# Layer 3 of a four-layer hybrid begins on image 0 before the layer ahead of it is done, without the dummy image

## What is computed

```python
x = x + _L0_conv_ref(_gn(x), ...)
x = x + _L1_conv_ref(_gn(x), ...)
t = _to_tokens(x)
t = t + _L2_attn_ref(_ln_t(t), L2_attn_w_attn, L2_attn_w_proj)
t = t + _L2_ffn_ref(_ln_t(t), L2_ffn_W1, L2_ffn_b1, L2_ffn_W2, L2_ffn_b2)
t = t + _L3_attn_ref(_ln_t(t), L3_attn_qkv_w, L3_attn_qkv_b, L3_attn_out_w, L3_attn_out_b)
t = t + _L3_ffn_ref(_ln_t(t), ...)
```

```python
for g in range(NUM_GROUPS):
    ag = x[g * gs:(g + 1) * gs]
    gamma = jnp.max(jnp.abs(ag))
    xq = xq.at[g * gs:(g + 1) * gs].set(jnp.clip(ag * QB / (gamma + EPS), -QB + EPS, QB - EPS))
```

## Time and profile before

| what | us |
|---|---|
| median of 3 runs | 804.9 |
| lowest and highest of them | 804.72 and 805.72 |
| the profiled execution | 806.04 |
| its span in the trace | 803.8 |
| PE busy | 743.9 (93%) |
| DVE busy | 578.1 |
| ACT busy | 571.6 |
| POOL busy | 253.1 |

### The profile page before, as it was taken

One profiled execution on the slowest core, in us unless ns is written; L12 is line 12 of the kernel. 1 busy time (PEld: TensorE's weight loads), 2 busy tenths in 40 slices (PEclk: granted clock), 3 DMA queues, 4 the chain that ended last, 5 costly groups with the idle time before them and its releaser, 6 DMA issues.

```text
span 803.8 us, 16948 instructions
## 1 busy us (share of the span) xinstructions
PE 743.9 (93%) x5265; PEld 583.6 (73%) x5265; DVE 578.1 (72%) x1415; ACT 571.6 (71%) x1425; POOL 253.1 (31%) x485
## 2 busy tenths in 40 slices
PE   1896999999999888999998986999999999999997
PEld 1874788788788776777776585677777786777775
DVE  6238677676777567788886798688888735877775
ACT  3323777977777557888886866688888748788785
POOL 1902155565554332121222000131212100544434
PEclk9999899999999999999999998899999959999999
DMA  6000000110110132333230002133333102223220
GB/s 218 1 1 0 1 7 17 20 16 18 20 17 16 26 90 74 90 90 104 80 103 17 0 1 80 51 99 88 102 94 89 29 1 82 50 59 76 63 50 20
DMA packets 60073, 41.36 MB, mean 51 GB/s; under 512 B 33904, under 2 KB 52464, under 8 KB 59888
## 3 DMA queue, kind: packets, MB, share of 16 engines
q1 hardware_dynamic: 60016, 40.63, 19.9%
HBM read 12.24 MB, written 3.21 MB: 19 GB/s over the span
## 4 chain that ended last, share of the span: by engine, by line
PE 77%; DVE 11%; ACT 4%; issue 3%; DMA 2%; SPq 2%; POOL 1%; POOLq 0%; DVEq 0%; ACTq 0%
PE ps L1236 11%; PE ps L990 10%; PE ps L1403 9%; PE ps L1418 8%; PE ps L1091 6%; PE ps L995 5%; PE ps L1075 3%; PE ps L1019 3%; PE ps L1033 3%; PE ps L998 2%; PE ps L1020 2%; SPq L309 2%; DMA qk<-hl 2%; PE ps L940 2%; DVE amax L1861 2%
## 5 line engine op out<-in xcount | busy, mean ns | idle before, releaser
L625 ACT ACTIVATE ee<-ps,nmax 128x128 f32<-128x128 f32 (+1 forms) x576 | 205.2, 445 | 11.5 <-DVE nmax L1592 6.4
L1236 PE MATMUL ps<-w,ee 128*128 128x128 f32 x960 | 134.8, 274 | 2.0 <-ACT big L612 1.9
L1236 PEld LDWEIGHTS ps<-w,ee 128*128 128x128 f32 x960 | 112.8, 143 | 13.6 <-ACT ee L625 2.8
L612 ACT ACTIVATE big<-ps 128x512 f32<-128x512 f32 (+1 forms) x192 | 96.6, 555 | 24.7 <-PE ps L1236 23.0
L1595 DVE TENSOR_REDUCE nmax<-ps 128x2 f32<-128x256 f32 x192 | 97.5, 550 | 13.5 <-PE ps L998 8.9
L1716 DVE TENSOR_TENSOR hhl<-ee,hhl 128x512 fp32r<-128x512 f32 x96 | 79.1, 829 | 33.1 <-ACT hhl L859 31.6
L990 PE MATMUL ps<-kh,big 128*128 128x256 f32 x384 | 94.7, 391 | 1.5 <-POOL big L385 1.2
L1592 DVE TENSOR_REDUCE nmax<-ps 128x4 f32<-128x1024 f32 x48 | 58.7, 1224 | 45.3 <-PE ps L990 45.1
L1403 PE MATMUL ps<-qk,w1hl 128*128 128x512 f32 x288 | 85.4, 405 | 0.0
L1418 PE MATMUL ps<-hhl,w2hl 128*96 128x512 f32 x288 | 82.4, 396 | 2.2 <-DVE big L1946 1.9
L529 POOL TENSOR_TENSOR xc<-big,xc 96x512 f32<-96x512 f32 x32 | 52.1, 1628 | 100.0 <-DVE big L1946 99.4
(11 more groups left out here) (260 smaller groups left out, 1333.2 us busy)
## 6 DMA issues: line engine op xcount, KB each, us to landing
qk<-hl SPq DMA_DIRECT2D x256, 96.0 KB, 3.1
big<-moe_gate SPq DMA_DIRECT2D x8, 768.0 KB, 6.9
w<-w_in SPq DMA_DIRECT2D x1, 1735.0 KB, 12.5
xc<-x_in SPq DMA_DIRECT2D x4, 384.0 KB, 5.6
l_mix<-on SPq DMA_DIRECT2D x32, 48.0 KB, 2.1
tok<-l_mix SPq DMA_DIRECT2D x16, 96.0 KB, 2.0
out<-xc SPq DMA_DIRECT2D x8, 192.0 KB, 2.1
w<-w_in SPq DMA_DIRECT2D x1, 998.0 KB, 8.8
```

The source lines that it names most:

```text
L612: nc.scalar.activation(et[:, h, 0:w], ps[:, 4 + hh, 0:w], ACT.Copy).then_inc(own(l, f"et{hh}"), 1)
L625: last = nc.scalar.activation(ee[:, ke, hh, qc, 0:w], src, ACT.Exp, bias=nmax[:, kp, hh, qc:qc + 1])
L1236: last = nc.tensor.transpose(ps[:, 4 + hh, b * P:(b + 1) * P], ee[:, u, hh, qc, tc * P:(tc + 1) * P], ident)
```

## The change

1. The five groups need not be through when layer 3 begins. Channels are now transposed and copied by 4 tiles (512 tokens, m = 0 to 7) rather than by half a group: m = 0 needs group 0 alone. m = 0 and 1 go through banks 0 and 1, the later ones all through bank 6. Steps of late groups are moved into layer 3's first units (`F2_LATE_PE`, `F2_LATE_ACT`, `F2_LATE_DVE`, by unit k): the quantise step of group 4 (f4) is in unit 0 on DVE, n4 in unit 2, the norms and roots of groups 3 and 4 on ACT in units 0 and 1, transposes m = 2 to 7 in units 0, 1, 2, 3 and 5.
2. The dummy image is gone in layers 2 and 3; its steps only count their semaphores up. So are the two matmuls that filled bank 6.
3. Image 0 of layer 3 is restacked by two queues: SP issues 4 of the 8 DMAs, ACT the other 4 (step D0, between the root and the norm of group 1).
4. The second matmul's results have banks of their own (`Y2_BANKS`), so that it waits for earlier ones only in group 4.
5. POOL begins `stage` in layer 3 once two pieces of `xn` are there, and does the cast and subtraction of `w2hl` after four images rather than two. Its all-reduces have a list of their own.

```diff
-F2_PE = ["h0", "h1", "h2", "h3", "h4", "y0", "y1", "y2", "y3", "T0", "Q0", "y4", "T1", "Q1", "S0", "T2", "S1", "T3", "V0", "T4"]
-F2_ACT = [..., "L0", "R0", "N0", "R1", "C0", "N1", "Q0", "R2", "N2", "C1", "Q1", "R3", "N3",
-          "C2", "R4", "X0", "C3", "C4"]
-F2_DVE = [..., "y0", "q4", "f0", "y1", "b0", "f1", "y2", "b1", "f2", "k0", "y3", "b2", "f3", "y4",
-          "k1", "b3", "m0", "f4", "n4", "m1", "v0"]
-Y2_BANKS = [(6, 7), (0, 1), (6, 2), (0, 1), (6, 2)]
+F2_PE = ["h0", "h1", "h2", "h3", "h4", "y0", "y1", "y2", "y3", "T0", "Q0", "y4", "Q1", "T1", "S0", "S1", "V0"]
+F2_ACT = [..., "L0", "R0", "N0", "C0", "Q0", "R1", "D0", "N1", "C1", "Q1", "R2", "N2", "X0"]
+F2_DVE = [..., "y0", "q4", "f0", "y1", "b0", "f1", "y2", "k0", "b1", "f2", "y3", "b2", "k1", "y4", "m0",
+          "f3", "m1", "v0"]
+F2_LATE_PE = {0: [2], 1: [3], 2: [4, 5], 3: [6], 5: [7]}
+F2_LATE_ACT = {0: ["C2", "R3"], 1: ["R4", "N3", "C3"], 2: ["C4", "C5"], 3: ["C6"], 5: ["C7"]}
+F2_LATE_DVE = {0: ["f4"], 1: ["b3"], 2: ["n4"]}
+Y2_BANKS = [(6, 7), (0, 1), (2, 3), (4, 5), (6, 3)]
...
-                stack(l, 0, 0)
-                stack(l, 1, 1)
+                for n in range(2):
+                    stack(l, n, n, (0,) if l == 3 and n == 0 else (0, 1))
...
             def outputs_to_sbuf(l, i):
+                if isinstance(i, int) and i < 0:
+                    act.sem_inc(own(l, "ot"), 1)
+                    return
...
+                    if l == 3 and isinstance(k, int) and k != 3:
+                        late(k)
...
+                        elif step[0] == "D":
+                            act.wait_ge(*upto(3, "hi", g + 1))
+                            for t, (h0, h1) in enumerate(((0, 0), (0, 1), (1, 0), (1, 1))):
+                                if t == 1:
+                                    act.wait_ge(*upto(3, "lo", g + 1))
+                                parts = hl[C // 2:C, g, :, :, :].rearrange("c a h x -> c (a h) x")[:, h0:h1 + 3:h1 + 2 - h0, :]
+                                nc.scalar.dma_start(qk[(4 + t) * HD:(5 + t) * HD, g, 3:9, :].bitcast(F32), parts.bitcast(F32)).then_inc(own(3, f"stacked{g}"), 16)
...
+            def ln3_transposes(m):
+                g = (2 * m + 1) // GI
                 if g < NG - 1:
                     pe.wait_ge(sg("ln3_normed_act"), g + 1)
                 else:
                     pe.wait_ge(sg("ln3_normed_dve"), 1)
+                if m < 2:
+                    pe.wait_ge(sg("f2_y2"), 4)
+                elif m == 2:
+                    pe.wait_ge(sg("f2_y2"), 2 * NG)
+                else:
+                    pe.wait_ge(sg("l3_xn"), m)
+                for t in range(4):
+                    last = nc.tensor.transpose(ps[0:C, ln3_bank(m), t * P:(t + 1) * P], on[:, 4 * m + t, :], ident)
+                last.then_inc(sg("ln3_t_ps"), 1)
...
                 if l == 3:
-                    pe.wait_ge(sg("f2_y2"), 2 * NG)
-                    mm(ps[0:C, 6, :], ident[:, 0:C], xn[:, B * N:(B + 2) * N], start=True, stop=True)
-                    pe.wait_ge(sg("l3_xn"), 2 * NG)
+                    pe.wait_ge(sg("f2_y2"), 8)
...
+                    if l == 3 and isinstance(k, int) and k == 3:
+                        for m in F2_LATE_PE[k]:
+                            ln3_transposes(m)
+                        pe.wait_ge(sg("l3_xn"), 7)
...
+                        if isinstance(i, int) and i == 0:
+                            pe.sem_inc(own(l, "av"), 1)
+                        else:
+                            weigh_values(l, npar, 0)
+                            weigh_values(l, npar, 1).then_inc(own(l, "av"), 1)
...
                             if g == 0:
                                 keys_ready(3, 0, 0, 0)
-                            pe.wait_ge(sg("f2_y2"), 2 * g + 8)
+                            if g == 0:
+                                pe.wait_ge(sg("l3_xn"), 2)
+                            else:
+                                pe.wait_ge(sg("f2_y2"), 2 * NG)
```

207 lines of the change are left out of this document (119 added, 88 removed).

## The result

| | before | changed |
|---|---|---|
| median of the runs made side by side, us | 804.8 (4 runs) | 814.3 (4 runs) |
| lowest and highest, us | 802.2 and 805.7 | 813.5 and 816.1 |
| ratio with 95% interval | | 1.0135 (1.0117 to 1.0153) |
| span in the trace, us | 803.8 | 812.4 |
| mean granted clock of PE | 0.973 | 0.961 |

The changed kernel is slower by 1.35%: 9.5 us between the medians, 10.9 by the ratio. I had forecast +2 us, with +4.7 as the end of my range. The sign was right, the size was not, and the page alone doesn't say why: PE is busy 1.6 us less than in the earlier trace rows, so the time went into waiting.

What follows compares the result with a forecast made beforehand. PE, busy 93% of the span, was taken as the limit. Layer 2's +0.7 us and layer 3's +1.3 for the clock made +2.0 on the median of 804.9: 806.9 us, range 803.4 to 809.6.

Steps and rivals of the forecast that it cites:

- Behind it PE is full again and both kernels do the same: Layer 3 behind image 0's weigh step: no difference between the kernels, so the comparison stopped at that step, 516.61 before.
- My term for the clock: Layer 3, PE pieces up to image 0's weigh step: half clock costs 0.3 to 2.9 us more, taken as +1.3.
- The pay-back of the lead: Layer 3's first units: the 10 us lead at image 2's projection is lost to late steps, weighing image 0 at 516.9.
- PE was not what was short: Layer 3: the dummy's work goes, but late steps still cost DVE 7 us and ACT about 9, wherever they stand.
- Rival 2: Layer 3: each of ACT's four DMA issues takes 1.15 us instead of 0.64, +3.3 on top, 810.2 us; chance 0.10.
- Rival 1: Waits are short enough that PE stays at 2.4 GHz: -1.7 us in layer 3, 0 in layer 2, 803.2; chance 0.20.
- Layer 2: Dropping the dummy gains 0 because PE waits for POOL's `xb`; clock risk, bounds -0.4 to +1.4, taken as +0.7 us.
- The wait of about 1 us for the restack of image 2: Layer 2: a sign of the forecast being right, PE waiting about 1 us for image 2's restack.
- Rival 3: The dummy was PE's load, POOL reaching `xb` sooner: 2.5 us less in layer 2, 1.3 more in layer 3, 803.7; chance 0.08.
- the +0.3 of the path: Layer 3: PE weighs image 0 at 516.9 against 516.61 before, +0.3 us.
- the +0.4 of the seventh transposes: Layer 3, two units behind image 0's weigh step: the seventh transposes, with nothing dropped beside them, add 0.4 us.
- my sign of being wrong in layer 2: Layer 2: the forecast is wrong if the second weigh step comes over 1 us earlier than before.

Runs made afterwards that it cites:

- experiment 2: The kernel before, with only POOL's cast and subtraction of the expert weights moved behind the outputs of images 0 and 1: 811.1 us, 1.0089 times before.
- 5: The changed kernel plus a one-column POOL subtraction that nobody reads, behind the copy of image 3's input, where POOL was idle: 808.1 us, 1.0057 times before.
- 4: The changed kernel with the cast and subtraction of the expert weights right behind POOL's last all-reduce of the feed-forward layer: 814.1 us, 1.0120 times before.
- 8: The changed kernel with the hidden one-column POOL subtraction, SP issuing all eight DMAs of image 0 and ACT none: 808.1 us, 1.0063 times before.
- 9: The changed kernel with the hidden one-column POOL subtraction, plus four unread PE matmuls in the waits of layer 3's units 2 and 3: 805.7 us, 1.0022 times before.
- experiment 12: The changed kernel with the hidden one-column POOL subtraction and late feed-forward steps reordered in ACT's and DVE's lists: 801.3 us, 0.9972 times before.
- 3: The kernel before without the dummy image in layer 2 alone, layer 3 as before: 802.6 us, 0.9988 times before.
- 7: The kernel before without the dummy image in both layers, nothing starting early: 802.1 us, 0.9988 times before.

## Why the prediction was wrong, step by step

- **"Behind it PE is full again and both kernels do the same"** is the step that failed. I compared the two kernels at the weigh step of image 0, and counted from layer 2's last weigh step I was near there: I forecast +1.3 us for layer 3, and the mark stands +1.6 later (80.66 against 79.03), which is about what such marks differ by without cause. In the trace's own time it even stands 1.3 us sooner (515.31 against 516.61). But behind it come +3.0 us up to image 1 and +7.2 up to image 2, and both kernels do not do the same.
- **The 7.2 us** are POOL's reload: PE's wait of 5.97, and half clock behind it (the weigh step of image 2 takes 2.49 instead of 1.50). My sum has no term for the move of the expert weights behind the outputs of images 0 and 1: it is 3.8 us of work (1.15 and 2.64) on an engine that is idle most of the time, and I passed over it. The row that would have warned me is POOL's 7.01 us ahead of the subtraction of `w2hl` (shown above), labelled as a wait for PE that had ended long before. I had no row of POOL in layer 3 at all among mine. Shown by experiment 2 (+7.2 us from that move alone, by the ratio) and 5 (the gap goes).
- **The 3.0 us** between images 0 and 1 are half clock (2.4 us: 11.25 against 8.87 in experiments 4, 8, 9 and 12) and a wait of 0.47 for the copy of the last block, which I had at 0.4. My term for the clock counted the pieces ahead of the weigh step of image 0 only; the half clock went on behind it. The term was mis-sized because of where I stopped to look. Whether these 2.4 us belong to the change in every execution stays open, since the clock of this piece differs between traces of kernels that are much alike.
- **The pay-back of the lead** went as I wrote it, at times up to 3 us sooner, as all of this trace is: the restacked keys arrived at 489.2 (I said 490.1), DVE idled 1.96 us for the root of group 2 (I said 2.0), image 2 was projected at 497.23 (499.8), the quantisation of group 4 filled 501.6 to 505.3 on DVE (504.3 to 508.1), ACT's norm of group 3 started at 506.66 (509.4), and the bank-6 hand-overs followed. What I took for the nature of the overlap ("PE was not what was short") was the order of the lists: experiment 12 takes the same steps in another order and wins 5.7 us up to image 1, 3.5 of them up to image 0. I had both facts in the sum, the idle DVE and the norm that waits behind `f4`, and read them as costs to add instead of as things that an order decides.
- **Rival 2**, a dear issue from ACT, is out: 0.67 us each, about what I took (0.64). **Rival 1**, a spared clock, did not come by itself. The Trainium skill's page "TensorE: Matmul & The Clock Gate", section "Why this matters for your kernels", which I weighed there, ties a fall of the clock in mid-kernel to longer gaps. Here the clock fell behind waits of 1.51, 2.17 and 1.47 us (transposes of 1.06 us at 511.62, against 0.61 at 509.54) and was still low in the weigh step (2.78 us), and the measurement decides.
- **Layer 2**: I said +0.7. The weigh step of image 0 came at the same distance behind layer 1, 18.0 us: POOL's `xb` is what PE waits for, as I said (0.92 us, where I had 1.6 or 1.5), and the clock fell, as I feared, but it had cost about as much before, a little earlier (the half clock of the earlier trace rows, which this trace doesn't have). The wait of about 1 us for the restack of image 2 that I gave as a sign did not come: PE takes those scores at 315.46 with no wait. The term belongs at 0, and with what follows it is probably a gain: experiments 3 and 7 have 0.9988, 1 us, with intervals that just reach 1. In the trace 1.0 of it is the last restack of layer 2, for which PE waited before (row below). The three profiled kernels with layer 2's dummy wait there 0.94 to 1.00 us, the others 0.35 or less. Why, no run tells.

```profile
426.42 0.61 PE L995 MATMUL ps<-qk 128*128 128x512 f32 x2 [1.00 <-DMA qk<-hl]
```

- **Rival 3**, the dummy as PE's load, gave 2.5 us for layer 2. Experiments 3 and 7 have 1.0 for one dummy and no more for both.
- **The sum**: +1.6 up to image 0, +3.0 and +7.2 behind it are +11.8 between the marks, as the table has it with rounding (107.5 less 95.7). The trace up to layer 2's last weigh step gives back 2.9 (437.58 less 434.65), of which 1.3 stood already at the end of layer 1. That leaves +8.9 at image 2, and +8.6 at the end of the span. My own sum has two slips that do not decide: the +0.3 of the path and the +0.4 of the seventh transposes are named and then in no line of it, unless in the +1.3, and the range begins at 803.4 where rival 1 has 803.2.
- **The side**: my chance of 0.51 for slower was on the right side largely by luck, for a reason that made up the smaller part of the loss. And my sign of being wrong in layer 2, a second weigh step over 1 us earlier, came (312.16 against 313.50) for no reason of the change: the trace was 1.3 us ahead at the end of layer 1 already.

## What to carry to other kernels

Before you move a step on an engine that is mostly idle, look at the idle time ahead of every instruction that it passes, and ask of each long one whether its releaser had really been late: a cost that belongs to whichever instruction comes first (here a reload of POOL behind the all-reduces) moves to the next in line. Put such a payment where the engine has nothing queued behind that others wait for, with a one-column instruction if need be. And when an overlap moves waits rather than removing them, try the order of the steps before you judge the overlap: five steps moved in the lists were worth 0.85% here (1.0057 to 0.9972).
